# Alternating weight transposes with projection passes in a cross-attention and mixture-of-experts kernel

## The reference

```
x  [32, 112, 256], ctx [32, 375, 192], 16 heads of 64
q = layernorm(x) @ Wq ; k, v = split(ctx @ Wkv)
a = softmax(q k^T / 8) @ v                  per head
x = x + (a @ Wproj + bproj)
h = layernorm(x)
p = softmax(h @ gate_w)                     8 experts, the 2 best kept, renormalised
out = x + sum_e p_e * (silu(h @ Wg_e) * (h @ Wu_e)) @ Wd_e     inner width 512
```

## Time and profile before

| | |
|---|---|
| median of 3 runs | 1475.11 us (1474.66 to 1478.47) |
| the profiled execution | 1475.41 us, span 1473.6 us |
| PE busy | 1432.4 us, 97% |
| PEld busy | 1266.3 us, 86% |
| DVE busy | 1058.9 us, 72% |
| ACT busy | 856.5 us, 58% |
| POOL busy | 624.7 us, 42% |
| mean granted clock of PE | 0.992 |

### The profile page before, as it was taken

The page is one execution under the profiler, slowest core; times in us unless marked ns, Lnnn a source line. Parts: engine busy times, 40 slices in busy tenths (PEclk is TensorE's granted clock), DMA queues, the critical chain, the costliest instruction groups (busy, mean ns, idle before and its releaser), DMA issues.

```text
span 1473.6 us, 38599 instructions
## 1 busy us (share of the span) xinstructions
PE 1432.4 (97%) x11960; PEld 1266.3 (86%) x11961; DVE 1058.9 (72%) x2868; ACT 856.5 (58%) x2392; POOL 624.7 (42%) x671
## 2 busy tenths in 40 slices
PE   6999999999999999999999999999997999999996
PEld 5888888888888888888888888888886788888885
DVE  5667777777777777777777777777768776666664
ACT  5566556555665566656655655556655555555553
POOL 2634344344545343545344443545436242333332
PEclk9999999999999999999999999999998899999998
DMA  9322222222222222322222222212128233333332
GB/s 262 108 68 69 75 73 74 67 76 67 73 67 73 73 80 78 94 82 68 73 67 73 74 73 70 73 38 73 28 64 314 50 66 56 55 52 57 51 57 26
DMA packets 101508, 114.75 MB, mean 78 GB/s; under 512 B 17276, under 2 KB 88172, under 8 KB 101356
## 3 DMA queue, kind: packets, MB, share of 16 engines
q1 hardware_dynamic: 88300, 95.25, 22.0%
q0 software_dynamic: 12144, 15.66, 5.9%
q10 hardware_dynamic: 1024, 3.34, 0.7%
HBM read 62.28 MB, written 51.93 MB: 78 GB/s over the span
## 4 chain that ended last, share of the span: by engine, by line
PE 87%; DVE 6%; DMA 3%; issue 2%; ACT 2%; DVEq 0%; ACTq 0%; POOLq 0%; SPq 0%
PE bank L1486 23%; PE bank L1429 22%; PE bank L1555 11%; PE bank L1531 10%; PE bank L1521 8%; PE bank L1576 6%; PE bank L1493 4%; DVE neg_max L1279 2%; DMA out<-y_out,dest_now 2%; PE bank L1731 2%; ACT prob L891 1%; DVE probT L1285 1%; PE bank L1684 1%; DVE Wgu L1138 1%; DMA WkU_whole<-in_L_xattn_Wkv 0%
## 5 line engine op out<-in xcount | busy, mean ns | idle before, releaser
L891 ACT ACTIVATE prob<-bank,neg_max 112x375 f32<-112x375 f32 x512 | 299.0, 589 | 133.7 <-DVE neg_max L1279 133.7
L1279 DVE TENSOR_REDUCE neg_max<-bank 112x1 f32<-112x375 f32 x512 | 244.0, 540 | 14.5 <-PE bank L1521 14.4
L1531 PE MATMUL bank<-ident,prob 112*125 112x112 f32 x1536 | 216.5, 273 | 6.5 <-ACT prob L891 2.4
L1531 PEld LDWEIGHTS bank<-ident,prob 112*125 112x125 f32 x1536 | 197.7, 188 | 20.0 <-ACT prob L891 14.0
L822 POOL DMA_INDIRECT out<-y_out,dest_now x63 | 97.8, 1553 | 200.4 <-DMA out<-y_out,dest_now 144.4
L1555 PEld LDWEIGHTS bank<-probT,V 125*64 125x64 f32 x3072 | 149.1, 137 | 39.0 <-issue 36.5
L1046 DVE TENSOR_TENSOR K_l<-bank,K_h 128x376 fp32r<-128x376 f32 x256 | 140.5, 550 | 56.9 <-ACT K_h L847 52.7
L1555 PE MATMUL bank<-probT,V 125*64 125x112 f32 x3072 | 176.6, 264 | 2.7 <-DVE probT L1285 1.9
L1429 PE MATMUL bank<-Wgu,hT_h 128*128 x504 | 166.6, 412 | 2.3 <-DVE hT_l L1347 2.2
L845 ACT COPY V<-bank 125x512 f32<-125x512 f32 x96 | 56.5, 588 | 164.3 <-PE bank L1493 161.7
L847 ACT CAST K_h<-bank 128x376 fp32r<-128x376 f32 x256 | 121.0, 473 | 31.7 <-PE bank L1486 29.4
(11 more groups left out here) (217 smaller groups left out, 4008.9 us busy)
## 6 DMA issues: line engine op xcount, KB each, us to landing
bins<-pad_rows SPq DMA_DIRECT2D x29, 1032.0 KB, 5.9
inv_rows<-sums SPq DMA_DIRECT2D x126, 128.0 KB, 2.9
h_in<-bins SPq DMA_DIRECT2D x63, 129.0 KB, 2.3
Wgu<-in_L_ffn_gate_up_w SPq DMA_DIRECT2D x6, 1024.0 KB, 7.0
y_sb<-in_ctx SPq DMA_DIRECT2D x32, 187.5 KB, 2.7
y_sb<-in_ctx SPq DMA_DIRECT2D x62, 93.8 KB, 2.7
x_sb<-in_x SPq DMA_DIRECT2D x16, 224.0 KB, 3.0
x_res<-in_x SPq DMA_DIRECT2D x32, 112.0 KB, 2.4
```

The costliest lines, as they stand in the source:

```text
L891: nc.scalar.activation(prob[:, j, :], S_ps[j][0:LQ, 0:LKV], ACT.Exp, bias=neg_max[:, j:j + 1], accum_out=row_sum[:, head // HB, head % HB: ...
L1279: nc.vector.tensor_reduce(neg_max[:, j:j + 1], S_ps[j][0:LQ, 0:LKV], AX.X, ALU.max, negate=True).then_inc(max_done, 1)
L1531: last = nc.tensor.transpose(S_ps[j][0:KR, t * LQ:t * LQ + LQ], prob[:, j, t * KR:t * KR + KR], ident[0:LQ, 0:LQ])
```

## The change

Five things are altered in the attention part.

1. In the third step PE makes six projection passes, then transposes of the weights and projection passes in turn (`turn_prob_and_project`): six pairs, the mid item, six pairs, and the last six passes. The count of instructions is the same.
2. The q products have other places: in the odd batch 0 and 1 in the first step, 2, 3, 4 in the second, third and fourth; in the even batch 5 and 6 in the first, 7 in the second. The fourth step has its item in "early" (q 4 or xT 1), the third in "mid". "late" is gone.
3. On DVE `residual` of the third step stands behind `turned(0)`, `turned(1)` and the mid item. Mean and variance (`moments`) are a function of their own and stand in the fourth step, behind the low parts of K and ahead of `turned(0)`.
4. `turn_hn` of the last batches moves behind the second block of transposes of the fourth step, `keep_hnT` behind `turned(1)`.
5. `gw_rows`, `weighed`, `multiplied` and `logits` lie where the first two experts' `Wd` come later, and that load (1 MB) is issued in the last pair instead of the one before.

```diff
-    q_at = {(1, 0): (0,), (1, 1): (1,), (1, 2): (2, 3), (1, 3): (4,), (0, 0): (5,), (0, 1): (6,), (0, 2): (7,)}.get((odd, s), ())
+    q_at = {(1, 0): (0, 1), (1, 1): (2,), (1, 2): (3,), (1, 3): (4,), (0, 0): (5, 6), (0, 1): (7,)}.get((odd, s), ())
...
-              "early": one if s < 2 else [],
-              "mid": one[:1] if s >= 2 else [],
+              "early": ones[:1] if s != 2 else [],
+              "mid": ones[1:] if s != 2 else ones,
...
             def residual(i, b, slot, bank):
...
+            def moments(b, slot):
+
                 dve.wait_ge(x2_done, b + 1)
                 nc.vector.bn_stats(stat2[:], x2[:, slot, :]).then_inc(st2, 1)
...
                         for k in of_K[1:]:
                             low_part(a, k)
+                        if s == 3 and there(b - 1, B):
+                            moments(b - 1, 1 - odd)
                         if s == 2 and there(b, B):
                             normalise(b, 0)
-                        if s == 2 and there(b - 1, B):
-                            residual(i, b - 1, 1 - odd, A_ps[1])
                         if there(b, B):
                             turned(b, s, 0)
                         for k in made_at["early"]:
                             low_part(a, k)
                         if there(b, B):
                             turned(b, s, 1)
+                        if s == 3 and there(b - 1, B) and not by_vector(b - 1):
+                            keep_hnT(b - 1, A_ps[1])
                         for k in made_at["mid"]:
                             low_part(a, k)
+                        if s == 2 and there(b - 1, B):
+                            residual(i, b - 1, 1 - odd, A_ps[1])
...
+            def turn_prob_and_project(b, s, k, bank):
+
+                n = (2 * k + 2) * KT
+                for j in (2 * k, 2 * k + 1):
+                    pe.wait_ge(exp_done, H * b + 4 * s + j + 1)
+                    for t in range(KT):
+                        turned = nc.tensor.transpose(S_ps[j][0:KR, t * LQ:t * LQ + LQ],
+                                                     prob[:, j, t * KR:t * KR + KR], ident[0:LQ, 0:LQ])
+                        if t == KT - 1:
+                            turned.then_inc(probT_made, 1)
+                        project_pass(bank, n // 3, n % 3)
+                        n += 1
...
-                            project(b - 1, A_ps[1])
-                        if s == 3 and there(b - 1, B) and not by_vector(b - 1):
-                            for k in a.at(odd, 2, "late") if a else []:
-                                pe.wait_ge(lo_done, a.split(k))
-                            turn_hn(b - 1, 1 - odd, A_ps[1])
-                        if there(b, B):
+                            pe.wait_ge(OT_lo, 2 * b)
+                            project_passes(A_ps[1], 0, 2 * KT)
+                            turn_prob_and_project(b, s, 0, A_ps[1])
+                        elif there(b, B):
                             turn_prob(b, s, 0)
...
+                        if s == 2 and there(b - 1, B):
+                            turn_prob_and_project(b, s, 1, A_ps[1])
+                            project_passes(A_ps[1], 3 * NJ - 2 * KT, 3 * NJ).then_inc(proj_made, 1)
+                        elif there(b, B):
                             turn_prob(b, s, 1)
+                        if s == 3 and there(b - 1, B) and not by_vector(b - 1):
+                            turn_hn(b - 1, 1 - odd, A_ps[1])
```

More of the change, by code:

```diff
@@ L109, in bank_of @@
         return int(a in SECOND)
-    return {"early": 1, "mid": 0 if s == 2 else 7, "late": 1}[place]
+    return {"early": 1, "mid": 0 if s == 2 else 7}[place]
 class Ahead:
@@ L330, in attention_and_experts @@
         early = 2
+        gw_rows = nc.alloc_sbuf_tensor_at("gw_rows", [LQ, C, E], F32, offset=wd_at)
+        place["at"] = wd_at
+        weighed = sb("weighed", [LQ, 2, C], F32)
+        multiplied = sb("multiplied", [LQ, E // 2, C], F32)
+        logits = sb("logits", [LQ, E], F32)
+        assert place["at"] <= wd_at + early * FJ * C * 4 and E <= early * FJ
         place["at"] = wd_at + early * FJ * C * 4
@@ L558, in pair @@
                         load_expert(sp, 0)
+                        sp.dma_start(Wd[:, 0:early].rearrange("p e k n -> p (e k) n"),
+                                     down_w[0:early].rearrange("e (k p) n -> p (e k) n", p=P)).then_inc(wd_early, 16)
                     if known(i) and i == NP - 1 and odd:
@@ L946, in pair @@
                             sum_experts(b - 2)
-                        for k in made_at["late"]:
-                            evacuate(a, k)
                         if known(b) and b == B - 1 and s == 3:
@@ L1323, in pair @@
                             mark(b - 2, odd)
-                        for k in made_at["late"]:
-                            low_part(a, k)
                         if s == 2 and there(b - 2, B):
@@ L1395, in four_tiles @@
                         residual(NP, B - 1, 1, C_ps)
+                        moments(B - 1, 1)
                     if known(t) and t == 2:
@@ L1566, in turn_last_inverses, with project_pass, project_passes @@
                 last.then_inc(inv_turned, 1)
-            def project(b, bank):
-                if known(b) and b == 0:
-                    pe.wait_ge(wp_done, 8)
-                for half in range(2):
-                    pe.wait_ge(OT_lo, 2 * b + half + 1)
-                    for j in range(HALF * half, HALF * half + HALF):
-                        for n, (w, m) in enumerate(((OT_h, WpH), (OT_h, WpL), (OT_l, WpH))):
-                            last = mm(bank[0:LQ, 0:C], w[:, j, :], m[:, j, :], start=j == 0 and n == 0,
-                                      stop=j == NJ - 1 and n == 2)
-                last.then_inc(proj_made, 1)
+            def project_pass(bank, j, n):
+                w, m = ((OT_h, WpH), (OT_h, WpL), (OT_l, WpH))[n]
+                return mm(bank[0:LQ, 0:C], w[:, j, :], m[:, j, :], start=j == 0 and n == 0, stop=j == NJ - 1 and n == 2)
+            def project_passes(bank, first, end):
+                for n in range(first, end):
+                    last = project_pass(bank, n // 3, n % 3)
+                return last
+            def project(b, bank):
+                pe.wait_ge(OT_lo, 2 * b + 1)
+                project_passes(bank, 0, 3 * HALF)
+                pe.wait_ge(OT_lo, 2 * b + 2)
+                project_passes(bank, 3 * HALF, 3 * NJ).then_inc(proj_made, 1)
+            def turn_prob_and_project(b, s, k, bank):
[9 more added lines that the diff above has]
+                        n += 1
             def count(b):
@@ L1625, in pair @@
                         for k in early:
+                            if s == 3 and there(b - 1, B):
+                                pe.wait_ge(x2_done, b)
                             make(a, k, i)
@@ L1652, in pair @@
                             context_product(a, k, True, False)
-                        for k in made_at["late"]:
-                            if there(b - 1, B):
-                                pe.wait_ge(x2_done, b)
-                            make(a, k, i)
                         if s == 0 and there(b - 2, B) and not by_vector(b - 2):
```

24 lines of the change are left out of this document (7 added, 17 removed).

## The result

The changed kernel is slower by 1.2%: 1494.28 us median of 5 runs (1492.41 to 1497.08) against 1476.74 us of the kernel before in the same comparison; the ratio is 1.0117, 95% interval 1.0099 to 1.0134. The forecast was 1482.2, with a range from 1469 to 1489. The direction was right, the size was not: the two profiled executions lie 17.0 us apart (1475.4 and 1492.4) where the sum had 6.8.

What follows compares the result with a forecast made beforehand. TensorE, busy 97% of the span, was taken to bound the kernel. From 1475.4 us, -1.9 for the full pairs, +0.2 for the first two batches and +8.5 for the last two gave 1482.2; range 1469 to 1489.

Steps and rivals of the forecast that it cites:

- The alternation: Third step on PE: a pass behind a transpose costs 0.106 us against 0.109, so -0.08 per pair, up to 0.43 either side.
- The second V product's wait: Fourth step on PE: moments delay the low part in the same bank, giving back 0.19 us odd and about 0.47 even.
- 14 pairs at -0.12: Steady part: -0.12 us per pair of batches over the 14 full pairs, put at -1.9 with rounding.
- half of the copies' row: Odd fourth step on DVE: the low part of q 4 starts 0.41 us after the first copy, at 580.55.
- Cover that holds: Fourth step: `hn` is ready 3.32 us after the statistics start, at 583.16; DVE's gate products in the kernel before start at 582.98.
- DVE ends the step some 0.2 later, ahead of the next maxima: End of the fourth step: DVE finishes only some 0.2 us later, still ahead of the next step's maxima.
- 0.5 later: End of the fourth step: were DVE 0.5 us later, PE would stall in every first step.
- `hn` is late by 0.5: Rival: `hn` late by 0.5 in each fourth step, or a turn costs 0.124; 1489 us or more, chance 0.10.
- Moved, not saved: q products: first steps get one more and the third one less, 0.66 us each, with nothing saved.
- the wait in batch 30: Fourth step of batch 30: PE waits for `hn`, some 2.4 us idle; with the moved q products batch 30 is +2.9.
- Batch 31 up to its last step: Batch 31's third step: POOL's split of expert 1 holds DVE's small instructions, ending at +2.6 us instead of -1.2.
- The rest: Batch 31's fourth step: `hn` is ready later and DVE's chain behind it, including the tile plan, moves by 3.0 us.

Runs made afterwards that it cites:

- experiment 5: Changed kernel without its alternation: in the third step all 24 passes come ahead of the transposes; 1496.33 us, 3.2 more than the changed kernel.
- Experiment 7: Changed kernel with one more wait: POOL, after the first row block of `hn`, waits for DVE's four gate products; 1486.91 us.
- experiment 6: Changed kernel with the fourth step's item (q 4, xT 1) back between the first V product and the second block of transposes; 1493.85 us.
- 8 (second kernel): Experiment 8's first kernel plus `normalise` ahead of the second q product's low part, and batch 31's third step and `turn_hn` as in the kernel before; 1508.03 us.
- experiment 2: Changed kernel with DVE's four gate products moved from the fourth step to the next batch's first step, behind `normalise`; 1530.12 us.
- the second trace: The changed kernel unaltered, run again on another chip: 1493.14 us against 1483.85 of the kernel before, ratio 1.0063.
- experiment 4: Changed kernel with the moments right behind the residual in the third step for batches 29 and 30 alone; 1486.34 us.
- experiment 8: Three cumulative kernels on the change with moments in the third step: POOL scatters before multiplying, 1512.62 us; `normalise` and `turn_hn` moved, 1508.03; POOL's multiplication waits for gate products, 1465.92.
- experiment 3: Changed kernel with the fourth step's moments behind both copies of the turned weights in place of ahead of them; 1536.52 us.

## Why the prediction was right and wrong

**Right: the gains on PE.** As forecast, the fourth step has blocks of 0.58 and 0.77, `weigh` stands 0.12 behind the count, and the second V product is released by the low part. The alternation was taken for -0.08 per pair and within its bounds; experiment 5 gives -0.19, a turn of 0.22 - 0.12 = 0.10 in place of 0.106. The second V product's wait was 0.10 odd and 0.39 even, taken as 0.19 and 0.47. Each is off by 0.1 at most. Two slips of the working change little: 14 pairs at -0.12 are -1.7 and not -1.9, and half of the copies' row of 0.91 is 0.45 and not 0.41.

**Wrong: "Cover that holds" and "DVE ends the step some 0.2 later, ahead of the next maxima".** This is the step that failed, twice over. First, the end of the gate products was compared in absolute time. PE's odd fourth step itself became 0.22 shorter, and the first product starts 0.17 behind the end of `hn` (586.93 against 586.76), which was not counted; so, waiting for `hn`, the products end some 0.6 later against the next step and not 0.2. Experiment 7 has that case: 0.69 into the first step instead of 0.09. Second, their durations were taken from the earlier trace rows, where POOL did no arithmetic beside them. In the change `hn` is formed right there, and `yB` and the four products took 0.45 + 0.22 + 0.35 = 1.02 longer; the part of `yB` is absorbed by the wait for `hn`, the 0.57 of the products is not. The room can now be read from five cases, by the start of the maxima in the first step and what PE's first block takes over 0.58 (experiments 7 and 6, the changed kernel odd and even, experiment 6 again): 1.21 and 0; 1.53 and 0.09; 1.74 and 0.28; 1.77 and 0.32; 1.96 and 0.52. In these cases every tenth above 1.45 costs a tenth. In the kernel before they start at 0.84, so the room was 0.6 us; they now start 0.9 later. The prediction's "0.5 later" was nearly the size of the room, but its own 0.2 was what it went by. As a rival, "`hn` is late by 0.5" stood in the last place, with a chance of 0.10 together with another.

**Missed: `weigh` waits for `normalise` in the even first step**, 0.19 per pair. The second q product's low part stands ahead of `normalise` on DVE. "Moved, not saved" counted PE's part of the moved product and not its low part's place in DVE's queue. Experiments 8 (second kernel) and 2 show it.

The overrun and this wait make 0.31 + 0.52 = 0.83 in the first steps (9.28 and 9.50 in place of 8.97 and 8.98); less 0.17 that the other steps gave beyond the forecast, the pair is at +0.54 instead of -0.12.

**The last batches: the wait in batch 30 right, the rest near its size by luck.** Batch 30 came at +4.2 where 2.9 stood: the wait for `hn` as worked out, and on top of it 1.15 us for `weigh` and the V product's tail at half clock. Here a stall of 2 us was not over when the wait was; in the second trace the clock fell earlier, and the fourth step took 13.87 in place of 12.59. Batch 31 up to its last step is +2.3 where 2.6 stood, but the instruction that POOL's split held was the cast ahead of `onehot`, not `onehot` and `chosen`: placed 1 us wrong; in the second trace of the same kernel it was held for 1.98 us instead of 3.22 and batch 31 up to its last step took 0.5 less than in the kernel before, so this term was right by luck. The rest is +3.3 where 3.0 stood, and that is luck too. The start of the tile plan moved by 4.6 us in the last step (from 4.41 to 8.99), and the stretch from the last step to the end differs by 2.7 between traces of the kernel before alone (347.35 and 344.63). And the prediction gave `hn` as the cause, while the new place of `turn_hn` behind the second block, which it had at nothing, is most of it: with `hn` early (experiment 4) the plan still starts at 8.11, with `turn_hn` back in its place (experiment 8) at 4.40.

**What holds what.** The traces show three degrees. POOL's TENSOR_TENSOR of 2.39 and 4.57 us held a DVE instruction on SBUF operands to its own end and up to 0.41 behind it (`yB` by 0.41, the cast by 0.02, the fourth product by 0.29). POOL's `hn`, a TENSOR_SCALAR of 1.24 us, added 0.21 to 0.45 to `yB` and one product, and left the next product alone. Instructions that read PSUM weren't held: a maximum keeps 0.54 and the copy of V 0.68 to 0.69 beside all of it. The Trainium skill, "SBUF — State Buffer", section "SBUF: two separate sides", has the pair of ports locked for a whole instruction by whoever comes first; the trace agrees for the first kind where POOL is written as first (`yB`, 2.39 us beside 2.39). The fourth product of experiment 8 is written as starting 0.57 before POOL's and was held all the same, which fits only if POOL's start is off by as much. For `hn` the trace doesn't agree: by that rule the product at 586.93, inside the second `hn` block (to 587.96), would have ended there and not at 587.57, and the next would not have taken 0.41.

## What to carry to other kernels

When a change moves an instruction on one engine, list what the *other* engines do beside its new place, and price both at the length that they have side by side, not at the length that they had alone. An engine that is busy 72% has little room in the one step where its work is bunched. Compare ends with the start of the step that needs them, which moves too. And where a collision depends on who comes first by a tenth of a microsecond, a wait that fixes the order is worth more than a better guess: one semaphore took 3 us off each pair (71.7 to 68.75) and 42 us off the whole (1508.03 to 1465.92, on two chips).

## What was not expected of the hardware

One DVE instruction of 0.42 us, started 0.57 ahead of POOL's multiplication by the trace, took 3.25. POOL's row scattering made no DVE instruction longer (`yB` 0.55, products 0.42 beside DMA_INDIRECT), unlike its arithmetic. And PE's clock fell to half in batch 30 behind waits of 2.13 and 0.58 us, over 1 us after the load was back, and stayed there for 3 us under full load, while the stalls of 0.2 to 0.5 us in experiments 3 and 8 left it at 1.00.
